# A transformer block on one core: another order of the work in a unit of attention heads

## The chip, the cores and the metric

The kernel runs on one core of a Trainium2 chip. The metric is the device time of one execution in microseconds (us). Three runs of the kernel before gave 312.1, 312.3 and 313.58 us; the median is 312.3.

## The reference

The input x has shape (32, 32, 256), cond (32, 256). What is computed, in float32:

```
x = x + conv(x)                # depthwise causal convolution over 32 lags, the filter is cond
ada = cond @ ada_w + ada_b     # six parts: shift1, scale1, gate1, shift2, scale2, gate2
x1 = layernorm(x) * (1 + scale1) + shift1
q, k, v = x1 @ qkv_w + qkv_b   # 16 heads of 128
o = softmax(q @ k.T * 128**-0.5) @ v       # for each batch element, 32 tokens by 32
x = x + gate1 * (o @ out_w + out_b)
x2 = layernorm(x) * (1 + scale2) + shift2
x = x + gate2 * (gelu(x2 @ ffn_w1 + ffn_b1) @ ffn_w2 + ffn_b2)
```

The conditioned block's own residual enters twice: the result is the sum of the convolved x and the block's output.

## The kernel before

Channels lie on the partitions (2 tiles of 128), tokens along the free dimension; the 1024 tokens are worked in two halves of 512. Every engine has its own list of instructions, written out by hand in the order in which it runs them, and the engines meet at semaphores. An instruction that waits holds up all that stands behind it on its engine.

**Precision.** A product is made of three fast matmuls: each operand is split into a high part and a low part (the remainder), and low x high, high x low and high x high are summed (`three`, lines 943 to 947; `v_tile`, 949 to 956). For weights ScalarE writes the high part (`high_parts`, line 348) and GpSimd (POOL) the low part (`low_parts`, line 297); for activations ScalarE writes the high part and VectorE (DVE) the low one.

**Units.** The attention is worked in eight units U = 0 to 7: four groups of four heads for each half of the tokens. A unit has twelve projection tiles (`project`, line 958): 0 to 3 are q of the four heads, 4 to 7 k, 8 to 11 v for four blocks of 128 tokens. Each is six matmuls of 512 columns into one of three PSUM banks in turn (`PB[j % 3]`), and ScalarE copies it out (`evac`, line 404). Then come the scores of all four heads (`scores`, line 995), the softmax on DVE with the exponentials on ScalarE (`softmax_front`, `exps`, `softmax_probs`, `softmax_transpose`), and, inside the next unit, the attention of each head (`attend`, line 1007) and its share of the output projection (`out_proj`, line 1023). Between the two, ScalarE writes the head's output high part (`o_high`, line 431) and DVE the low part (`o_low`, line 668). Attention output has two banks, so heads 2 and 3 wait for the `o_low` of heads 0 and 1.

**What is fitted between.** Unit 0 is projected in two chunks while the second half's convolution still runs on DVE (`conv`, line 538, spread over units 0 to 2). Unit 1 also holds the rest of the product ada (`modulation`, `modulation_turned`). Units 3 and 5 hold a layernorm each, of 512 tokens: TensorE's `mean`, `var` and `spread` (lines 886, 904, 918), which share the scores' bank; DVE's `centre`, `scale_up`, `var_eps`, `norm`, `shift`; ScalarE's `squares` and `x1_high`; and POOL's `rstd` (line 301), on which `spread` waits. The mean takes its input in two parts, `mean_high` by ScalarE and `mean_low` by DVE. Unit 7 is followed by the first ffn layer (`ffn1`, line 1116; its gelu and high part are ScalarE's `hidden`, line 489; its low parts `hidden_low` go to DVE for odd tiles and to POOL for even ones). Among the ffn1 tiles stands the attention of unit 7, then the layernorm of the second half, `mean(4)`, which needs `residual(1)` (line 675) on DVE first.

**Weights.** SyncE issues their transfers in one order (lines 242 to 245): q, k, v of a unit and then its rows of out_w, each as soon as POOL has made the low parts of what lay in that place before.

The order of TensorE's work in a unit is in lines 1077 to 1114, and of its counterparts in 320 to 328 (POOL), 455 to 487 (ScalarE) and 722 to 826 (DVE).

Of the kernel before, what the change touches and what calls it, by code (L numbers as in the profile page):

```python
# [16 lines left out]
def cond_resid_block_kernel(nc, x, cond, ada_w, ada_b, qkv_w, qkv_b, out_w, out_b,  # L17
# [7 lines left out]
    CT = C // P  # L25
    INNER = out_w.shape[0]
    NH = INNER // P
    GH = 4
# [42 lines left out]
    with ExitStack() as ctx:  # L71
# [204 lines left out]
        def _(g):  # L276
# [43 lines left out]
            for U in range(1, NU):  # L320
                if U == 3:
                    rstd(2)
                if U == 5:
                    rstd(3)
                low_parts(U + 1, 0)
                low_parts(U + 1, 1)
                low_parts(U, 3)
                low_parts(U + 1, 2)
# [16 lines left out]
        def _(a):  # L345
# [109 lines left out]
            for U in range(1, NU):  # L455
                for j in range(4):
                    evac(U, j)
                if U == 1:

                    a.wait_ge(s_adap, 3)  # L460
                    a.wait_ge(s_adax, 1)
                    a.activation(ada_rows[:, :], S_BANK[:, 0:2 * P], ACT.Copy).then_inc(s_adac, 1)
                o_high(U - 1, 0)
                o_high(U - 1, 1)
                if U == 3:
                    squares(2)
                if U == 5:
                    squares(3)
                evac(U, 4)
                o_high(U - 1, 2)  # L470
                high_parts(U + 1, 0)
                o_high(U - 1, 3)
                if U == 3:
                    x1_high(2)
                if U == 5:
                    x1_high(3)
                for j in (5, 6, 7, 8):
                    evac(U, j)
                    if U in (2, 4) and j in (6, 7):
                        mean_high(U // 2 + 1, j - 6)  # L480
                high_parts(U + 1, 1)
                exps(U)
                evac(U, 9)
                high_parts(U, 3)
                evac(U, 10)
                evac(U, 11)
                high_parts(U + 1, 2)
# [11 lines left out]
            hidden(0, 0)  # L499
            hidden(0, 1)  # L500
            o_high(NU - 1, 0)
            hidden(0, 2)
            o_high(NU - 1, 1)
            hidden(0, 3)
            o_high(NU - 1, 2)
            o_high(NU - 1, 3)
            high_parts(NU, 3)
# [22 lines left out]
        def _(v):  # L530
# [195 lines left out]
            conv(1, 7, 9)  # L726
# [3 lines left out]
            conv(1, 9, 10)  # L730
            o_low(0, 2)
            conv(1, 10, 11)
            o_low(0, 3)
# [3 lines left out]
            conv(1, 11, 18)  # L737
# [3 lines left out]
            conv(1, 18, 20)  # L741
# [3 lines left out]
            conv(1, 20, 21)  # L745
            o_low(1, 2)
            conv(1, 21, 22)
            o_low(1, 3)
            conv(1, 22, len(DVE_LAGS[1]))
            mean_low(2)  # L750
            softmax_front(2)
            softmax_probs(2)
            softmax_transpose(2)

# [5 lines left out]
            o_low(2, 2)  # L760
            o_low(2, 3)
            norm(2)
            shift(2)
            x1_low(2)
            softmax_front(3)
# [5 lines left out]
            residual(0)  # L771
            mean_low(3)
            softmax_front(4)
            softmax_probs(4)
            softmax_transpose(4)

# [5 lines left out]
            o_low(4, 2)  # L782
            o_low(4, 3)
            norm(3)
            shift(3)
            x1_low(3)
            softmax_front(5)
# [5 lines left out]
            residual_sum(0)  # L793
            softmax_front(6)
            softmax_probs(6)
            softmax_transpose(6)

# [12 lines left out]
            hidden_low(0, 1)  # L810
            o_low(7, 0)
            o_low(7, 1)
            hidden_low(0, 3)
            o_low(7, 2)
            o_low(7, 3)
            residual(1)
# [39 lines left out]
        def _(pe):  # L856
# [216 lines left out]
            project_chunk(1, range(0, 5))  # L1073
            scores(0)
            project_chunk(1, (5,))

            for U in range(1, NU):

                ln = {3: 2, 5: 3}.get(U)
                if U == NG:  # L1080
                    pe.wait_ge(s_lo, CT * NC)
                project(U, range(0, 3))
                if U == 1:
                    pe.wait_ge(s_sd, U)
                    pe.wait_ge(s_adaw[1], 16)
                    modulation(1)
                    modulation(2)
                if ln:
                    pe.wait_ge(s_sd, U)
                    mean(ln)  # L1090
                project(U, (3,))
                attend(U - 1, 0)
                attend(U - 1, 1)
                project(U, (4,))
                if U == 1:
                    modulation_turned(1)
                    modulation_turned(2)
                attend(U - 1, 2)
                if ln:
                    var(ln)  # L1100
                out_proj(U - 1, 0)
                attend(U - 1, 3)
                out_proj(U - 1, 1)
                if ln:
                    spread(ln)
                out_proj(U - 1, 2)
                out_proj(U - 1, 3)
                project(U, (5, 6, 7, 8))
                if ln:
                    pe.wait_ge(s_mod, CT * (ln + 1))  # L1110
                if U == 1:
                    pe.wait_ge(s_adat, ADA_STEPS[2])
                scores(U)
                project(U, (9, 10, 11))
# [44 lines left out]
            ffn1(0, (0, 1, 2))  # L1159
            attend(last, 0)  # L1160
            attend(last, 1)
            ffn1(0, (3,))
            attend(last, 2)
            out_proj(last, 0)
            attend(last, 3)
            for h in (1, 2, 3):
                out_proj(last, h)
            ffn1(0, (4, 5, 6, 7))
# [63 lines left out]
```

## Time and profile before

| | |
|---|---|
| median of three runs | 312.3 us |
| profiled execution | 311.81 us |
| its span, first instruction to last | 310.0 us |
| TensorE busy | 298.0 us, 96% |
| VectorE busy | 180.2 us, 58% |
| ScalarE busy | 174.5 us, 56% |
| GpSimd busy | 120.4 us, 39% |

How to read it: PE is TensorE's matmuls, PEld its weight loads, DVE VectorE, ACT ScalarE, POOL GpSimd, SP SyncE. Matmuls are pipelined and their ends are modelled, so records of successive matmuls overlap, and the pace is read from their starts. L945 is line 945 of the kernel; a helper's line stands for all its calls. In timelines, like instructions in a row are merged into one with a count (x16), and an instruction before which the engine was idle has in brackets for how long and what released it.

### The profile page before, as it was taken

How to read it: one execution, taken by the hardware profiler on the slowest of the kernel's cores; microseconds unless marked ns; L12 is line 12 of the kernel's file. 1: busy time of each engine (PE TensorE's matmuls, PEld its weight loads, DVE VectorE, ACT ScalarE, POOL GpSimd, SP SyncE). 2: the span in 40 equal slices, each digit the busy share in tenths (PEclk: the TensorE clock that was granted, in tenths of full speed). 3: DMA queues.
4: the chain of work that ended last, by engine and by line, in shares of the span. 5: the costliest groups of instructions: out<-in, count | busy, mean ns of one | idle time of the engine just before them, and what ended most of it. 6: DMA issues, size and time to landing. Idle time of an engine off the chain costs nothing.

```text
span 310.0 us, 6149 instructions
## 1 busy us (share of the span) xinstructions
PE 298.0 (96%) x2604; PEld 251.9 (81%) x2604; DVE 180.2 (58%) x303; ACT 174.5 (56%) x316; POOL 120.4 (39%) x103
## 2 busy tenths in 40 slices
PE   4978999999999999999999999999999999899995
PEld 3875997878898888788888888888898888678885
DVE  3997698987866745472546554341620556957232
ACT  5752568434762855486376736644762794625901
POOL 5007729331911544072337305531821671611400
PEclk9999999999999999999999999999999999999999
DMA  7903321400160061007004300610150020000012
GB/s 231 362 27 79 112 84 57 150 0 2 43 231 0 2 229 45 0 4 271 1 2 153 120 2 2 213 59 2 59 212 2 2 68 3 0 0 3 0 68 68
DMA packets 15259, 23.00 MB, mean 74 GB/s; under 512 B 792, under 2 KB 8320, under 8 KB 15232
## 3 DMA queue, kind: packets, MB, share of 16 engines
q1 hardware_dynamic: 15184, 22.58, 21.6%
q8 instruction: 20, 0.33, 0.4%
q10 hardware_dynamic: 48, 0.03, 0.1%
q14 instruction: 7, 0.06, 0.1%
HBM read 21.57 MB, written 1.05 MB: 73 GB/s over the span
## 4 chain that ended last, share of the span: by engine, by line
PE 85%; DVE 9%; POOL 3%; ACT 1%; DMA 1%; issue 1%; DVEq 0%; POOLq 0%
PE bank L945 18%; PE bank L947 18%; PE bank L946 18%; PE bank L1019 9%; DVE xc L548 6%; PE bank L953 5%; PE bank L954 4%; PE bank L955 4%; PE bank L1003 3%; POOL wl L294 3%; PE bank L925 1%; DVE x1l L617 1%; PE bank L894 1%; DMA crow<-in_cond_dram 1%; PE bank L867 1%
## 5 line engine op out<-in xcount | busy, mean ns | idle before, releaser
L294 POOL TENSOR_TENSOR wl<-raw,wh 128x512 fp32r<-128x512 f32 x72 | 98.7, 1398 | 133.2 <-ACT wh L357 116.5
L408 ACT ACTIVATE pool<-bank,bT 128x512 f32<-128x512 f32 x56 | 38.5, 688 | 54.3 <-PE bank L947 54.3
L945 PE MATMUL bank<-x1h,wl 128*128 128x512 f32 (+1 forms) x176 | 66.3, 377 | 0.8 <-DVE x1l L623 0.4
L947 PE MATMUL bank<-x1h,wh 128*128 128x512 f32 (+1 forms) x176 | 65.1, 370 | 0.0
L946 PE MATMUL bank<-x1l,wh 128*128 128x512 f32 (+1 forms) x176 | 65.1, 370 | 0.0
L671 DVE SCALAR_TENSOR_TENSOR ol<-bank,bT,oh 128x512 fp32r<-128x512 f32 x32 | 24.0, 750 | 36.6 <-ACT oh L433 35.6
L357 ACT ACTIVATE wh<-raw 128x512 fp32r<-128x512 f32 x72 | 40.9, 621 | 3.5 <-PE bank L947 3.5
L548 DVE SCALAR_TENSOR_TENSOR xc<-x,condT,xc 128x496 f32<-128x496 f32 (+27 forms) x82 | 42.8, 592 | 0.1
L945 PEld LDWEIGHTS bank<-x1h,wl 128*128 128x128 f32 x176 | 33.2, 188 | 7.1 <-DVE x1l L623 0.8
L947 PEld LDWEIGHTS bank<-x1h,wh 128*128 128x128 f32 x176 | 33.2, 188 | 5.7
L946 PEld LDWEIGHTS bank<-x1l,wh 128*128 128x128 f32 x176 | 33.2, 189 | 5.4
L1019 PEld LDWEIGHTS bank<-pt,pool 128*128 128x128 f32 x256 | 32.1, 191 | 2.0 <-issue 0.3
L1019 PE MATMUL bank<-pt,pool 128*128 128x128 f32 x256 | 32.5, 275 | 0.0
L433 ACT ACTIVATE oh<-bank,bT 128x512 fp32r<-128x512 f32 x32 | 22.0, 686 | 10.0 <-PE bank L1019 10.0
L945 PE MATMUL bank<-oh,wl 128*128 128x512 f32 x64 | 26.8, 418 | 0.2 <-DVE ol L671 0.2
L953 PE MATMUL bank<-wh,x1l 128*128 128x512 f32 x64 | 25.9, 404 | 0.0
L947 PE MATMUL bank<-oh,wh 128*128 128x512 f32 x64 | 25.1, 392 | 0.0
L946 PE MATMUL bank<-ol,wh 128*128 128x512 f32 x64 | 25.0, 390 | 0.0
L954 PE MATMUL bank<-wl,x1h 128*128 128x512 f32 x64 | 24.9, 389 | 0.0
L955 PE MATMUL bank<-wh,x1h 128*128 128x512 f32 x64 | 24.9, 389 | 0.0
L643 DVE TENSOR_REDUCE mx<-bank 128x16 f32<-128x512 f32 x8 | 5.5, 692 | 32.4 <-PE bank L1003 32.4
L666 DVE STREAM_TRANSPOSE pt<-pnorm 32x512 f32<-32x512 f32 (+1 forms) x36 | 23.2, 644 | 1.2
(121 smaller groups left out, 421.5 us busy)
## 6 DMA issues: line engine op xcount, KB each, us to landing
raw<-in_L_cond_qkv_w_dram SPq DMA_DIRECT2D x24, 512.0 KB, 5.6
raw<-in_L_cond_out_w_dram SPq DMA_DIRECT2D x8, 512.0 KB, 3.7
raw<-in_L_cond_ffn_w_dram SPq DMA_DIRECT2D x4, 512.0 KB, 5.1
adaw<-in_L_cond_ada_w_dram SPq DMA_DIRECT2D x1, 1024.0 KB, 10.8
out_dram<-pool SPq DMA_DIRECT2D x3, 256.0 KB, 2.2
pool<-in_x_dram SPq DMA_DIRECT2D x2, 256.0 KB, 3.1
adaw<-in_L_cond_ada_w_dram SPq DMA_DIRECT2D x1, 512.0 KB, 5.4
pool<-in_x_dram SPq DMA_DIRECT2D x1, 512.0 KB, 6.2
```

The costliest lines, as they stand in the source:

```text
L294: g.tensor_tensor(wl[:, cols], raw[:, cols], wh[:, cols].bitcast(F32), ALU.subtract)\
L357: a.activation(wh[:, cols], raw[:, cols], ACT.Copy).then_inc(s_whi[i], 1)
L408: a.activation((q_sb if j < GH else k_sb)[:, j % GH, :], src, ACT.Identity, bias=bias(U, j // GH, j % GH)).then_inc(s_ev, 1)
L548: m = v.scalar_tensor_tensor(out=acc[:, :, j:], in0=xs[:, :, :T - j], scalar=w, in1=(acc if i else xs)[:, :, j:], op0=ALU.mult, op1=ALU.add)
L671: v.scalar_tensor_tensor(out=ol[:, h, :], in0=OB[h % 2][:, :], scalar=bT[:, row:row + 1], in1=oh[:, h, :].bitcast(F32), op0=ALU.add, op1=A ...
L945: pe.matmul(dst, wl[:, w_cols], a_hi, start=start, stop=False)
L946: pe.matmul(dst, wh[:, w_cols], a_lo, start=False, stop=False)
L947: return pe.matmul(dst, wh[:, w_cols], a_hi, start=False, stop=stop)
L953: pe.matmul(dst, x1l[:, kt, tk], wh[:, wc], start=(kt == 0), stop=False)
L954: pe.matmul(dst, x1h[:, kt, tk], wl[:, wc], start=False, stop=False)
L955: m = pe.matmul(dst, x1h[:, kt, tk], wh[:, wc], start=False, stop=(kt == CT - 1))
L1019: m = pe.matmul(OB[h % 2][:, t * P:(t + 1) * P], v_sb[:, t, h * P:(h + 1) * P], pt[:, h, t, :], start=True, stop=True)
```

## The change

All of it is order; no operation is added or taken away, and no tile or semaphore changes.

- **TensorE, a unit:** attention of heads 2 and 3 of the last unit moves behind projection tile 7, directly ahead of this unit's scores; the output projection of all four heads stands in one piece behind the scores; v's tiles 8 to 11 come last. `mean` stands behind tile 3, `var` behind tile 4, `spread` behind tile 6. In unit 0 the scores stand behind the fourth tile of the second chunk, not the fifth. In the last part, ffn1's tiles 1 and 2 stand between heads 0, 1 and heads 2, 3, and tiles 3 to 7 behind the output projection.
- **ScalarE:** the same order for its copies; `mean_high` moves into units 3 and 5, behind `evac` of tiles 0 and 1; `squares` stands between `o_high` of heads 0 and 1; `exps` ahead of the k weights' high parts; in unit 1 the copy of ada's rows stands behind `evac` 5.
- **DVE:** in units 3 and 5 `o_low` of heads 2 and 3 stands behind the layernorm; `residual(0)` and `mean_low(3)` behind the softmax of unit 4, `mean_low(2)` behind that of unit 2; `hidden_low(0, 3)` ahead of `residual(1)`.
- **POOL:** `low_parts(U + 1, 0)` stands ahead of `rstd`.

```
@@ POOL
             for U in range(1, NU):
+                low_parts(U + 1, 0)
                 if U == 3:
                     rstd(2)
                 if U == 5:
                     rstd(3)
-                low_parts(U + 1, 0)
                 low_parts(U + 1, 1)
                 low_parts(U, 3)
                 low_parts(U + 1, 2)
@@ ScalarE
                 for j in range(4):
                     evac(U, j)
-                if U == 1:
-                    a.wait_ge(s_adap, 3)
-                    a.wait_ge(s_adax, 1)
-                    a.activation(ada_rows[:, :], S_BANK[:, 0:2 * P], ACT.Copy).then_inc(s_adac, 1)
+                    if U in (3, 5) and j < CT:
+                        mean_high((U + 1) // 2, j)
                 o_high(U - 1, 0)
-                o_high(U - 1, 1)
                 if U == 3:
                     squares(2)
                 if U == 5:
                     squares(3)
+                o_high(U - 1, 1)
                 evac(U, 4)
-                o_high(U - 1, 2)
                 high_parts(U + 1, 0)
-                o_high(U - 1, 3)
+                evac(U, 5)
+                if U == 1:
+                    a.wait_ge(s_adap, 3)
+                    a.wait_ge(s_adax, 1)
+                    a.activation(ada_rows[:, :], S_BANK[:, 0:2 * P], ACT.Copy).then_inc(s_adac, 1)
+                evac(U, 6)
+                evac(U, 7)
                 if U == 3:
                     x1_high(2)
                 if U == 5:
                     x1_high(3)
-                for j in (5, 6, 7, 8):
-                    evac(U, j)
-                    if U in (2, 4) and j in (6, 7):
-                        mean_high(U // 2 + 1, j - 6)
+                o_high(U - 1, 2)
+                o_high(U - 1, 3)
+                exps(U)
                 high_parts(U + 1, 1)
-                exps(U)
+                evac(U, 8)
                 evac(U, 9)
                 high_parts(U, 3)
...
             hidden(0, 0)
+            o_high(NU - 1, 0)
+            o_high(NU - 1, 1)
             hidden(0, 1)
-            o_high(NU - 1, 0)
-            hidden(0, 2)
-            o_high(NU - 1, 1)
-            hidden(0, 3)
             o_high(NU - 1, 2)
             o_high(NU - 1, 3)
+            hidden(0, 2)
+            hidden(0, 3)
             high_parts(NU, 3)
@@ DVE
-            conv(1, 7, 9)
+            conv(1, 7, 8)
             o_low(0, 0)
             o_low(0, 1)
-            conv(1, 9, 10)
-            o_low(0, 2)
-            conv(1, 10, 11)
-            o_low(0, 3)
+            conv(1, 8, 10)
             modulation(1)
             modulation(2)
             one_plus(2, SCALE2)
-            conv(1, 11, 18)
+            conv(1, 10, 11)
+            o_low(0, 2)
+            o_low(0, 3)
             softmax_front(1)
...
             centre(2)
             o_low(2, 0)
             o_low(2, 1)
             scale_up(2)
             var_eps(2)
-            o_low(2, 2)
-            o_low(2, 3)
             norm(2)
             shift(2)
             x1_low(2)
+            o_low(2, 2)
+            o_low(2, 3)
...
-            hidden_low(0, 1)
             o_low(7, 0)
             o_low(7, 1)
-            hidden_low(0, 3)
+            hidden_low(0, 1)
             o_low(7, 2)
             o_low(7, 3)
+            hidden_low(0, 3)
             residual(1)
             mean_low(4)
@@ TensorE
-            project_chunk(1, range(0, 5))
+            project_chunk(1, range(0, 4))
             scores(0)
-            project_chunk(1, (5,))
+            project_chunk(1, (4, 5))
...
-                project(U, range(0, 3))
+                project(U, range(0, 4))
...
                     mean(ln)
-                project(U, (3,))
                 attend(U - 1, 0)
                 attend(U - 1, 1)
                 project(U, (4,))
+                if ln:
+                    var(ln)
+                project(U, (5, 6))
                 if U == 1:
                     modulation_turned(1)
                     modulation_turned(2)
-                attend(U - 1, 2)
-                if ln:
-                    var(ln)
-                out_proj(U - 1, 0)
-                attend(U - 1, 3)
-                out_proj(U - 1, 1)
                 if ln:
                     spread(ln)
-                out_proj(U - 1, 2)
-                out_proj(U - 1, 3)
-                project(U, (5, 6, 7, 8))
+                project(U, (7,))
+                attend(U - 1, 2)
+                attend(U - 1, 3)
...
                 scores(U)
-                project(U, (9, 10, 11))
+                for h in range(GH):
+                    out_proj(U - 1, h)
+                project(U, (8, 9, 10, 11))
...
-            ffn1(0, (0, 1, 2))
+            ffn1(0, (0,))
             attend(last, 0)
             attend(last, 1)
-            ffn1(0, (3,))
+            ffn1(0, (1, 2))
             attend(last, 2)
-            out_proj(last, 0)
             attend(last, 3)
-            for h in (1, 2, 3):
+            for h in range(GH):
                 out_proj(last, h)
-            ffn1(0, (4, 5, 6, 7))
+            ffn1(0, (3, 4, 5, 6, 7))
             mean(4)
```

## Rows read from the trace of the kernel before

**Rows 1.** The page, part 1: busy time, share, instructions of each engine.
```profile
PE 298.0 (96%) x2604; PEld 251.9 (81%) x2604; DVE 180.2 (58%) x303; ACT 174.5 (56%) x316; POOL 120.4 (39%) x103
```

**Rows 2.** Stretches: units 2 and 3; length, busy times, granted clock, DMA share, GB/s.
```profile
80.56:107.34 26.78, 26.78 (x257) 22.57 (x256) 18.73 (x38) 16.05 (x27) 10.70 (x9) 1.00 0.24 80
107.34:136.79 29.45, 29.45 (x286) 24.80 (x285) 15.50 (x26) 17.25 (x30) 11.62 (x10) 1.00 0.21 73
```

**Rows 3.** Timeline of TensorE in unit 3: start, us, what.
```profile
113.55 0.39 PE L947 MATMUL bank<-x1h,wh 128*128 128x512 f32 x1
113.78 1.95 PE L1019 MATMUL bank<-pt,pool 128*128 128x128 f32 x16
115.48 0.48 PE L945 MATMUL bank<-x1h,wl 128*128 128x512 f32 x1
115.79 0.40 PE L946 MATMUL bank<-x1l,wh 128*128 128x512 f32 x1
116.03 0.39 PE L947 MATMUL bank<-x1h,wh 128*128 128x512 f32 x1
...
122.27 1.05 PE L925 MATMUL bank<-ident,rs 128*128 128x128 f32 x8
```

**Rows 4.** Timeline of ScalarE in unit 3.
```profile
114.87 0.69 ACT L433 ACTIVATE oh<-bank,bT 128x512 fp32r<-128x512 f32 x1 [0.20 <-PE bank L1019]
115.76 0.69 ACT L433 ACTIVATE oh<-bank,bT 128x512 fp32r<-128x512 f32 x1 [0.21 <-PE bank L1019]
116.35 1.14 ACT L388 ACTIVATE x<-yacc 128x512 f32<-128x512 f32 x2
...
118.61 1.14 ACT L357 ACTIVATE wh<-raw 128x512 fp32r<-128x512 f32 x2
```

**Rows 5.** Timeline of DVE in unit 3.
```profile
112.62 1.28 DVE L578 TENSOR_TENSOR yacc<-xc,bank 128x512 f32<-128x512 f32 x2 [2.52 <-PE bank L894]
115.59 1.65 DVE L671 SCALAR_TENSOR_TENSOR ol<-bank,bT,oh 128x512 fp32r<-128x512 f32 x2 [1.69 <-ACT oh L433]
117.15 1.28 DVE L585 TENSOR_TENSOR yacc<-yacc,adaT 128x512 f32<-128x512 f32 x2
...
118.98 0.17 DVE L597 TENSOR_SCALAR ve<-vt 128x4 f32<-128x4 f32 x1
```

**Rows 6.** Timeline of POOL in unit 3.
```profile
119.23 1.01 POOL L304 TENSOR_TENSOR rs<-ve,mhalf 128x4 f32<-128x4 f32 x1 [7.16 <-DVE ve L597]
120.21 2.53 POOL L294 TENSOR_TENSOR wl<-raw,wh 128x512 fp32r<-128x512 f32 x2
```

**Rows 7.** Line L585 by itself (ns min/median/max), and DVE and POOL at 262 us.
```profile
L585 DVE TENSOR_TENSOR yacc<-yacc,adaT x6: 412/684/1487, 25.2 to 117.7; 128x256 f32<-128x256 f32 x4, 128x512 f32<-128x512 f32 x2
...
262.23 2.39 DVE L685 TENSOR_TENSOR yacc<-yacc,xc 128x512 f32<-128x512 f32 x2
...
262.33 3.44 POOL L294 TENSOR_TENSOR wl<-raw,wh 128x512 fp32r<-128x512 f32 x2 [6.67 <-ACT wh L357]
```

**Rows 8.** Timelines of ScalarE and TensorE around the scores of unit 0.
```profile
47.45 0.83 ACT L420 ACTIVATE pool<-bank,bT 128x256 f32<-128x256 f32 x2
...
48.40 1.30 PE L1003 MATMUL bank<-pool 128*32 128x32 f32 x128
...
51.61 0.50 PE L945 MATMUL bank<-x1h,wl 128*128 128x512 f32 x1 [0.35 <-POOL wl L294]
```

**Rows 9.** Timelines of DVE and TensorE in unit 1.
```profile
64.29 3.08 DVE L548 SCALAR_TENSOR_TENSOR xc<-x,condT,xc 128x352 f32<-128x352 f32 x2
...
68.08 0.50 PE L945 MATMUL bank<-oh,wl 128*128 128x512 f32 x1 [0.18 <-DVE ol L671]
```

**Rows 10.** Timelines of ScalarE and TensorE ahead of mean(4).
```profile
262.92 0.69 ACT L494 ACTIVATE pool<-bank,bT 128x512 f32<-128x512 f32 x1
...
264.18 1.14 ACT L393 ACTIVATE x1h<-yacc 128x512 fp32r<-128x512 f32 x2
...
268.15 0.70 PE L894 MATMUL bank<-x1h,ones_r 128*128 128x512 f32 x2 [1.19 <-DVE x1l L617]
```

**Rows 11.** The page, part 6: size of a transfer, us from issue to landing.
```profile
raw<-in_L_cond_qkv_w_dram SPq DMA_DIRECT2D x24, 512.0 KB, 5.6
```

More of the change, by code:

```diff
@@ L457, in _ @@
                     evac(U, j)
+                    if U in (3, 5) and j < CT:
+                        mean_high((U + 1) // 2, j)
+                o_high(U - 1, 0)
+                if U == 3:
+                    squares(2)
+                if U == 5:
+                    squares(3)
+                o_high(U - 1, 1)
+                evac(U, 4)
+                high_parts(U + 1, 0)
+                evac(U, 5)
                 if U == 1:
@@ L462, in _ @@
                     a.activation(ada_rows[:, :], S_BANK[:, 0:2 * P], ACT.Copy).then_inc(s_adac, 1)
-                o_high(U - 1, 0)
-                o_high(U - 1, 1)
[L465 to L469, printed above, removed]
-                o_high(U - 1, 2)
-                high_parts(U + 1, 0)
-                o_high(U - 1, 3)
+                evac(U, 6)
+                evac(U, 7)
                 if U == 3:
@@ L740, in _ @@
             softmax_transpose(1)
-            conv(1, 18, 20)
+            conv(1, 11, 20)
             o_low(1, 0)
             o_low(1, 1)
-            conv(1, 20, 21)
+            conv(1, 20, 25)
             o_low(1, 2)
-            conv(1, 21, 22)
             o_low(1, 3)
-            conv(1, 22, len(DVE_LAGS[1]))
-            mean_low(2)
             softmax_front(2)
@@ L753, in _ @@
             softmax_transpose(2)
+            conv(1, 25, len(DVE_LAGS[1]))
+            mean_low(2)
             centre(2)
@@ L770, in _ @@
                 o_low(3, h)
-            residual(0)
-            mean_low(3)
             softmax_front(4)
@@ L775, in _ @@
             softmax_transpose(4)
+            residual(0)
+            mean_low(3)
             centre(3)
@@ L781, in _ @@
             var_eps(3)
-            o_low(4, 2)
-            o_low(4, 3)
             norm(3)
@@ L786, in _ @@
             x1_low(3)
+            o_low(4, 2)
+            o_low(4, 3)
             softmax_front(5)
@@ L792, in _ @@
                 o_low(5, h)
-            residual_sum(0)
             softmax_front(6)
@@ L796, in _ @@
             softmax_transpose(6)
+            residual_sum(0)
             for h in range(GH):
```

## The prediction

> **What bounds the kernel.** I read the busy shares first [rows 1]: TensorE is busy 96% of the span, no other engine above 58%. Then stretches of one unit each [rows 2]: an ordinary unit is 26.78 us long and TensorE is busy for all of it; a unit with a layernorm piece lasts 29.45 us, busy throughout; the granted clock is 1.00 (2.4 GHz) in both. Then TensorE's own timeline in unit 3 [rows 3]: two 512-column matmuls follow each other at 0.23 us (115.79 to 116.03), so a projection tile, an output-projection head or an ffn1 tile (six matmuls) takes 1.36 us. The attention of two heads takes 115.79 - 113.55 - 2 x 0.227 = 1.79 us, 0.90 a head. The scores take 1.44 us: 26.78 less twelve tiles and four heads of output projection (16 x 1.36), and less four heads of attention (3.58). So the loop has no idle time to win. TensorE waits only at a few edges, and a change of order can pay only there; everywhere else it can only open waits.
>
> The waits that there are: a recorded idle time counts from a modelled end, 0.39 after a matmul's start where the next starts after 0.23, so 0.16 is added, and 0.11 where the first matmul behind it takes 0.50. That gives 0.62 us for weight low parts before unit 1 [rows 8], 0.45 in unit 1 for o_low of head 3 [rows 9], and 1.35 ahead of mean(4), behind the last unit [rows 10]: 2.4 us together.
>
> **Units without a layernorm piece.** The same matmuls in another order; what each waits for is earlier than its new place. I count t from a unit's first tile. In the changed order tiles 0 to 3 end at 5.44, attention 0 and 1 at 7.23, tile 4 at 8.59, 5 and 6 at 11.31, 7 at 12.67, attention 2 and 3 at 14.46, scores at 15.90, output projection at 21.34, tiles 8 to 11 at 26.78. ScalarE takes a finished tile 0.20 us later and needs 0.69 [rows 4], so k's last tile is copied at 13.56, before the scores at 14.46. o_high and o_low of head 3 end near 15.4 and 16.2; the output projection of head 3 starts at 19.98. The softmax gets more time than before: the next attention is 16 us behind the scores, where it was 10. Joining heads 2, 3 and the scores gives nothing back, since the 26.78 us are full. What a change between the kinds of matmul costs I bound by the 0.09 us by which the first behind attention is recorded longer (0.48 for 0.39): term 0, bounds -0.6 and +0.6 for seven units.
>
> The weights' transfers are a matter of SyncE's order: the q transfer for unit U+1 is queued behind the o transfer, which waits for POOL's low_parts(U-1,3), and that moves with tile 9 to the end of unit U-1. In unit 3 it is issued about t = 2.4 and lands in 5.6 us [rows 11], at about 8; its first reader, high_parts(4,0), comes at 10.3. Term 0, but the cover is only 2 us.
>
> **Start and unit 1.** scores(0) moves ahead of chunk 1's fifth tile, and needs the evacuation of its fourth. ScalarE has high_parts(1,0) ahead of that, so the evacuation runs 47.45 to 48.28, and the scores start at 48.40 even now [rows 8]. They can't come earlier; the fifth tile (1.36 us) that fills this time now follows them, so unit 1 is reached 1.36 us later, less the 0.62 us wait for low parts, which are then ready: +0.74. In unit 1 the copy of ada_rows moves behind the evacuation of tile 4, high_parts(2,0) and the evacuation of tile 5 (0.20 + 0.6 + 1.0 + 0.6 behind tile 4), and with the copy, taken as half an evacuation, ends just after TensorE has made two more tiles (2.72) and wants to turn it: +0.1. The wait for o_low 3, caused by a conv pair of 3.08 us ahead of it, goes: -0.45. Term: +0.4, bounds -0.5 (the scores' wait goes unpaid) and +1.5.
>
> **Units 3 and 5, the largest term.** Here mean, var and spread stand between the tiles, and two edits make a chain that was covered late: PE's order, and on POOL low_parts(U+1,0) ahead of rstd. With t from the unit's first tile:
> - tiles 0 to 3 to 5.44; mean to 6.35; attention 0 and 1 to 8.14; tile 4 to 9.50; var (0.8) to 10.3; tiles 5 and 6 to 13.0: this is where spread stands. Before, two tiles and three heads of attention stood between mean and var (5.4 us; now a tile and two heads, 3.15), and two heads of output projection and one of attention between var and spread (3.6; now two tiles, 2.7).
> - ScalarE [rows 4]: o_high 0 starts 1.09 after the first attention (114.87 less 113.78), 7.44; squares 8.03 to 9.17 (centre ends 1.5 after mean [rows 5], 7.85, in time); o_high 1 9.07 to 9.76; evacuation of tile 4 9.70; high_parts(U+1,0) at 10.29, its first half at 10.9.
> - DVE [rows 5]: o_low 0 8.2; o_low 1 9.8 to 10.5; scale_up from 10.46, two operations at 0.6; var_eps behind it.
> - POOL [rows 6]: low_parts(U+1,0) can start at 10.99; its two operations take 2.53 alone. rstd (1.01) now stands behind them; before it stood ahead (119.23, then 120.21).
>
> Alone, POOL ends the low parts at 13.52 and rstd at 14.5: spread waits 1.6 us. But they collide with scale_up. What the rows show: L585, the same operation, takes 0.68, its half-size form 0.41, and once 1.49, where POOL subtracts beside it; the residual's two additions take 2.39 for 2 where 1.3 is usual, with POOL's low parts beside them [rows 7]. So each of the two waits for the other's whole operation: scale_up 0 to 11.1, low part 1 to 12.4, scale_up 1 to 13.0, low part 2 to 14.3, rstd to 15.3, spread at 15.4 in place of 13.0. The wait is 2.4 us in each of two units: +4.8. Bounds: +0.7, if POOL came to rstd as soon as ve is there (scale_up ends 11.8 alone, ve 12.2, rstd 13.3, spread 0.35 late, twice), and +7, if the weights came late and POOL held rstd behind them (another 1 us each). Behind spread nothing more is late: norm needs 1.5 us, tile 7 and two heads cover 3.15. The mean itself is close: mean_high now runs in this unit, and mean_low 1, which may wait for POOL's low_parts(U,2), ends near 5.3 for 5.44.
>
> The Trainium skill (SBUF: State Buffer, "Who interferes with whom") says that a DVE instruction with two SBUF inputs and a GpSimd instruction that reads SBUF exclude each other for the whole instruction, the first to start winning. That speaks against this change; by it the term is 4.8, and if two inputs did not contend it would be 3.2. The trace sides with the rule, by the row of L585.
>
> **The last unit.** I count from ffn1's first tile. Before, tile 3 stands ahead of attention 2; now tiles 3 to 7 stand behind the output projection. Tile 0, two heads, two tiles, two heads and the output projection end at 13.1; tile 3 at 14.5; its gelu and copy run from 14.7 to 16.1 (262.92 to 264.18 is the same pair [rows 10]). On DVE hidden_low(0,3) stands ahead of residual(1) and needs this copy; before, the residual began as soon as the output projection ended. So: hidden_low to 16.8, the two gating operations to 18.1, the two additions with POOL's low_parts(8,3) beside them (first half ready at 16.7, since high_parts(8,3) also stands behind hidden(0,3)) to 20.7, mean_high 1 to 21.3, mean_low to 23.2 with hidden_low of POOL beside it; mean at 23.3. TensorE has finished tile 7 at 20.0: a wait of 3.3 in place of 1.35. Term: +1.9; bounds -0.5 (nothing collides: mean at 20.9) and +3.
>
> **Sum.** 0.4 + 4.8 + 1.9 = 7.1 us on a profiled execution of 311.81 us (span 310.0 and 1.8 around it): 318.9. The median of the three runs is 0.5 above the profiled one: I say **319.0 us**.
>
> **Rivals.**
> - *The collisions don't bite.* POOL's operations slip between DVE's. For it: the middle record of L585 is 0.68 although POOL is busy 39% of the span. Against: the one at 1.49 [rows 1, 7]. 0.4 + 3.2 + 0 = 3.6: 315.5 us. Chance 0.2.
> - *The waits are longer.* POOL's low parts wait for a late q transfer with rstd behind them, or the clock falls in a wait of 2 to 3 us (the page shows full speed through the wait of 1.35; each us at 1.2 GHz would cost half a us). 2 to 4 us more: 321 to 323. Chance 0.1.
> - *Nothing changes.* TensorE stays full since rstd is in time after all. For it: before, spread had 2.0 us to spare (rstd ends at 120.24, spread starts at 122.27) [rows 3, 6]. Against: the new order takes more than that. 311.5 to 313. Chance 0.08.
> - *Faster.* One mechanism: the waits of before are closed by the tiles now behind them and none opens. It decides at ScalarE's high_parts(U+1,0): if POOL's low parts were through before var, near 10, rstd would be free; they would have to start 3.5 us earlier than I place them. Price: -2.4 us, 310. Chance 0.07.
>
> **How the numbers follow.** Forecast 0.55, its own range 317.2 to 320.5. A measurement tells 0.5% (1.6 us) from no change. Slower holds the forecast and the first two rivals, 0.85; no change 0.08; faster 0.07. The range goes down to the rival without collisions and up into the longer waits: 314.3 to 321.6; what lies outside is no change, faster and the upper part of the second rival, 0.2.
>
> **What would show it.** Right: in units 3 and 5 spread (L925) waits for POOL's rs by 2 to 2.5 us, POOL does two wl operations right ahead of rs, one scale_up takes 1.5 us or more; scores(0) waits 1.3 us for ScalarE's evacuation; mean(4) waits about 3.3 us for x1l, and residual(1) starts only after hidden_low(0,3). Wrong: rs ready ahead of spread; a TensorE wait in ordinary units, or ahead of every scores; or the loop's unit shorter than 26.78 us.

## The result

The changed kernel takes 320.38 us (median of 4, 319.86 to 321.41), the kernel before 312.25 (median of 4): ratio 1.026, 95% interval 1.0237 to 1.0283. Slower, as forecast; 319.0 was said, in a range of 314.3 to 321.6. Ratios here and below leave out executions over 1.5% longer than the fastest of the same kernel; that concerns two of e3's six.

### The profile page after: what moved, and what is told of

It is laid out like the page before. It is cut to its first block, busy times and chain, and to the rows that moved or that the text cites. A ratio compares the mean times of both kernels' runs of the same rounds, so it can differ in the third digit from the quotient of the medians.

```text
span 318.0 us, 6149 instructions
## 1 busy us (share of the span) xinstructions
PE 301.0 (95%) x2604; PEld 254.7 (80%) x2604; DVE 189.9 (60%) x303; ACT 173.8 (55%) x316; POOL 122.8 (39%) x103
## 4 chain that ended last, share of the span: by engine, by line
PE 82%; DVE 11%; ACT 3%; POOL 2%; DMA 1%; issue 1%; DVEq 0%; POOLq 0%
PE bank L945 18%; PE bank L946 17%; PE bank L947 17%; PE bank L1019 9%; DVE xc L550 5%; PE bank L953 5%; PE bank L955 5%; PE bank L954 5%; PE bank L1003 3%; PE bank L925 1%; POOL wl L294 1%; DVE yacc L687 1%; PE bank L894 1%; POOL rs L304 1%; ACT oh L433 1%; DMA crow<-in_cond_dram 1%
## 5 line engine op out<-in xcount | busy, mean ns | idle before, releaser
L294 POOL TENSOR_TENSOR wl<-raw,wh 128x512 fp32r<-128x512 f32 x72 | 101.0, 1426 | 147.0 <-ACT wh L357 130.3
L550 DVE SCALAR_TENSOR_TENSOR xc<-x,condT,xc 128x496 f32<-128x496 f32 (+27 forms) x82 | 44.5, 615 | 0.1
L411 ACT ACTIVATE pool<-bank 128x512 f32<-128x512 f32 x28 | 16.7, 596 | 34.6 <-PE bank L955 34.6
L1019 PEld LDWEIGHTS bank<-pt,pool 128*128 128x128 f32 x256 | 30.9, 191 | 1.7 <-issue 0.6
L1019 PE MATMUL bank<-pt,pool 128*128 128x128 f32 x256 | 31.3, 275 | 0.0
L945 PE MATMUL bank<-oh,wl 128*128 128x512 f32 x64 | 25.8, 403 | 0.0
L953 PE MATMUL bank<-wh,x1l 128*128 128x512 f32 x64 | 25.0, 391 | 0.0
```

The source lines that it names most:

```text
L294: g.tensor_tensor(wl[:, cols], raw[:, cols], wh[:, cols].bitcast(F32), ALU.subtract)\
L550: m = v.scalar_tensor_tensor(out=acc[:, :, j:], in0=xs[:, :, :T - j], scalar=w, in1=(acc if i else xs)[:, :, j:], op0=ALU.mult, op1=ALU.add)
L945: pe.matmul(dst, wl[:, w_cols], a_hi, start=start, stop=False)
L953: pe.matmul(dst, x1l[:, kt, tk], wh[:, wc], start=(kt == 0), stop=False)
L1019: m = pe.matmul(OB[h % 2][:, t * P:(t + 1) * P], v_sb[:, t, h * P:(h + 1) * P], pt[:, h, t, :], start=True, stop=True)
```

## The profile after

The profiled execution took 319.86 us, its span 318.0, 8.0 more than before. First the page: the span and the busy shares.

```profile
span 318.0 us, 6149 instructions
PE 301.0 (95%) x2604; PEld 254.7 (80%) x2604; DVE 189.9 (60%) x303; ACT 173.8 (55%) x316; POOL 122.8 (39%) x103
```

The instructions are as many on every engine as before [rows 1]; TensorE is busy 3.0 us longer and idle 5.0 us longer. So 5 us are waits; the other 3 are longer records of the same matmuls: 1.6 at a lower clock behind the last unit, as the third stretch below shows, and 1.1 in the convolution's matmuls at the start (L881, 17.1 before and 18.2 now), which cost nothing, since the first v tile comes no later. The longest waits of TensorE (in total, times, longest):

```profile
PE bank L925 <- POOL rs L304: 4.2, 3, 1.9
...
PE bank L894 <- DVE x1l L619: 2.9, 1, 2.9
PE bank L1003 <- ACT pool L420: 1.3, 1, 1.3
```

The stretches by unit (columns as in [rows 2]): unit 2, unit 3 and the first 3.5 us of ffn2.

```profile
80.95:107.75 26.80, 26.80 (x257) 22.85 (x257) 23.09 (x44) 15.12 (x25) 12.59 (x10) 1.00 0.23 80
107.75:139.50 31.75, 29.84 (x286) 24.78 (x286) 19.90 (x27) 18.06 (x32) 12.16 (x10) 1.00 0.20 68
275.50:279.00 3.50, 3.50 (x10) 2.72 (x9) 2.99 (x5) 3.07 (x6) 1.29 (x1) 0.51 0.00 0
```

An ordinary unit is as long and as full as before; unit 3 has about 2 us in which TensorE stands. In the third row it is busy throughout, but at half its clock: 0.51 of full speed, that is, at the lower of its two levels (1.2 and 2.4 GHz).

Taken between the same instructions of both traces, the 8.0 us are: ahead of the first v tile of chunk 0 (TensorE's first L953, at 38.41 before and 38.33 after) -0.1; from it to unit 1 +0.82 (13.20 to 14.02); unit 1 -0.50; units 2, 4, 6 and 7 -0.10 together; unit 3 +2.20, unit 5 +2.39; unit 7's end to ffn2 +1.76; ffn2 to the end +1.56.

**Unit 3.** ScalarE, then DVE, then POOL, then TensorE, from each one's timeline (start, length, what, idle time before):

```profile
117.29 0.69 ACT L408 ACTIVATE pool<-bank,bT 128x512 f32<-128x512 f32 x1
117.87 1.14 ACT L357 ACTIVATE wh<-raw 128x512 fp32r<-128x512 f32 x2
```
```profile
117.36 0.75 DVE L673 SCALAR_TENSOR_TENSOR ol<-bank,bT,oh 128x512 fp32r<-128x512 f32 x1 [0.86 <-ACT oh L433]
118.02 2.39 DVE L587 TENSOR_TENSOR yacc<-yacc,adaT 128x512 f32<-128x512 f32 x2
120.34 0.30 DVE L596 STREAM_TRANSPOSE vt<-bank 128x128 f32<-128x128 f32 x1
120.68 0.90 DVE L599 TENSOR_SCALAR ve<-vt 128x4 f32<-128x4 f32 x1
```
```profile
118.57 2.98 POOL L294 TENSOR_TENSOR wl<-raw,wh 128x512 fp32r<-128x512 f32 x2 [7.05 <-ACT wh L357]
121.66 1.01 POOL L304 TENSOR_TENSOR rs<-ve,mhalf 128x4 f32<-128x4 f32 x1
```
```profile
122.72 1.16 PE L925 MATMUL bank<-ident,rs 128*128 128x128 f32 x8 [1.91 <-POOL rs L304]
```

POOL's two low parts start 0.55 us after DVE's scale_up and run beside it: scale_up takes 2.39 where it took 1.28 [rows 5], the low parts 2.98 where they took 2.53 [rows 6], and the reciprocal root (L304) stands behind both. Spread waits 1.91 as recorded, 2.07 by the reading of the prediction, which adds 0.16 to a recorded wait. The 0.90 us of ve, 0.17 before [rows 5], also end only when POOL's second low part does, at 121.6.

**Behind the last unit.** DVE, POOL, ScalarE and TensorE:

```profile
267.75 0.69 DVE L807 TENSOR_TENSOR hl<-pool,hh 128x512 fp32r<-128x512 f32 x1 [6.74 <-ACT hh L499]
268.36 1.40 DVE L682 SCALAR_TENSOR_TENSOR yacc<-bank,bT,adaT 128x512 f32<-128x512 f32 x2
269.68 3.42 DVE L687 TENSOR_TENSOR yacc<-yacc,xc 128x512 f32<-128x512 f32 x2
273.02 1.47 DVE L619 TENSOR_TENSOR x1l<-yacc,x1h 128x512 fp32r<-128x512 f32 x2
```
```profile
268.31 2.55 POOL L294 TENSOR_TENSOR wl<-raw,wh 128x512 fp32r<-128x512 f32 x2 [5.48 <-ACT wh L357]
270.82 1.73 POOL L332 TENSOR_TENSOR hl<-pool,hh 128x512 fp32r<-128x512 f32 x1
```
```profile
267.08 0.63 ACT L499 ACTIVATE hh<-pool 128x512 fp32r<-128x512 f32 x1
...
273.13 0.63 ACT L393 ACTIVATE x1h<-yacc 128x512 fp32r<-128x512 f32 x1 [1.06 <-DVE yacc L687]
```
```profile
274.63 0.70 PE L894 MATMUL bank<-x1h,ones_r 128*128 128x512 f32 x2 [2.87 <-DVE x1l L619]
275.17 0.68 PE L894 MATMUL bank<-x1l,ones_r 128*128 128x512 f32 x2
275.64 0.63 PE L945 MATMUL bank<-hh,wl 128*128 128x512 f32 x1
276.07 0.63 PE L946 MATMUL bank<-hl,wh 128*128 128x512 f32 x1
```

DVE has been idle for 6.74 us when it does hidden_low(0,3) (L807), because that waits for ScalarE's copy (L499) at 267.7; the residual (L682, L687) queues behind it, though its heads were ready (in e2 below it starts at 264.42), and its two additions then meet POOL's second low part and POOL's hidden_low (L332): 3.42 us. Mean(4) waits 3.03 (1.35 before [rows 10]). On DVE hidden_low(0,3) stood ahead of residual(1) in the kernel before too, but there its tile came ahead of attention 2. It is TensorE's move of tile 3 behind the output projection that made the copy late. From 275.64 on, 1 us behind the wait's end, the matmuls follow at 0.43 us, not 0.23: the clock has fallen. Eight do so: 8 x 0.2 = 1.6 us, the +1.56.

**Start.** The scores of unit 0 on TensorE:

```profile
48.25 1.30 PE L1003 MATMUL bank<-pool 128*32 128x32 f32 x128 [1.26 <-ACT pool L420]
```

The 1.26 us are the ScalarE evacuation that was foreseen.

## The experiments

The time of an execution varies with the stretch ahead of the first v tile and with the clock (the kernel before alone took 311.72 to 314.56 us in the 57 executions taken beside these runs); where a wait decides I read it in the trace, and lengths from the first v tile on. Ratios are to the kernel before on the same chip.

**1. e1_rstd_first: POOL's order alone undone.**
```
 for U in range(1, NU):
-    low_parts(U + 1, 0)
     if U == 3: rstd(2)
     if U == 5: rstd(3)
+    low_parts(U + 1, 0)
```


> The changed kernel with one edit undone: POOL's rstd stands ahead of low_parts(U+1,0) again. Theory (POOL's order holds rstd, and its low parts beside scale_up make ve late as well): POOL is idle until ve, which comes at about 119.8 instead of 121.6; rstd ends near 120.9, spread waits about 0.3 us instead of 2.07 in units 3 and 5, and the time falls by 3.5 us to about 316.9. Rival (TensorE's order alone brings var and spread too early; ve is late by DVE's own chain, rstd only follows it): the waits stay near 2 us and the time near 320.4.

Measured: 317.06 us, ratio 1.0141 (1.0103 to 1.018). DVE, POOL and TensorE in unit 3:
```profile
120.60 1.28 DVE L587 TENSOR_TENSOR yacc<-yacc,adaT 128x512 f32<-128x512 f32 x2
...
122.14 0.17 DVE L599 TENSOR_SCALAR ve<-vt 128x4 f32<-128x4 f32 x1
```
```profile
122.39 1.01 POOL L304 TENSOR_TENSOR rs<-ve,mhalf 128x4 f32<-128x4 f32 x1 [8.30 <-DVE ve L599]
123.37 2.52 POOL L294 TENSOR_TENSOR wl<-raw,wh 128x512 fp32r<-128x512 f32 x2
```
```profile
123.45 1.16 PE L925 MATMUL bank<-ident,rs 128*128 128x128 f32 x8
```
The root comes as soon as ve is there, scale_up and ve are short again, and spread stands only 0.33 us longer than its neighbours (0.45 - 0.23 after the last matmul's start, 0.11 in the first behind it). So POOL's place for the root, and the collision it brings, hold nearly all of this term; units 3 and 5 stay 0.35 and 0.56 longer than before.

**2. e4_before_low_first: the same edit put into the kernel before.**
```
 for U in range(1, NU):
+    low_parts(U + 1, 0)
     if U == 3: rstd(2)
     if U == 5: rstd(3)
-    low_parts(U + 1, 0)
```


> The kernel before with one edit of the change: low_parts(U+1,0) ahead of rstd on POOL. Theory (the price of POOL's order depends on how much stands between var and spread on TensorE, 3.6 us here): high_parts allow the first low part at 119.3, rstd starts near 121.9 and ends near 122.9, spread, due at 122.27, waits 0.6 to 0.7 us in units 3 and 5; the time rises by 1.3 us to about 313.6. Rivals: POOL's order by itself costs the whole 2.1 us a unit (316.4), or nothing, since TensorE's order is all (312.3).

Measured: 313.73 us, ratio 1.005 (1.0026 to 1.0075). Spread in unit 3:
```profile
122.94 1.16 PE L925 MATMUL bank<-ident,rs 128*128 128x128 f32 x8 [0.44 <-POOL rs L304]
```
Recorded 0.44 is 0.6 of wait, and the unit is 0.7 longer: that is what POOL's edit costs in the old order. The rest of the change without it (e10) makes units 3 and 5 longer by 0.35 and 0.55, both together by 2.2 and 2.4, about twice the sum. TensorE's new order has taken the cover: spread was due 14.8 us after the unit's first tile, 2.0 behind the end of the root; now it is due at 13.1.

**3. e5_no_collision: scale_up ahead of o_low 1, so that it is through before POOL starts.**
```
 o_low(2, 0)
-o_low(2, 1)
 scale_up(2)
+o_low(2, 1)
 var_eps(2)
```
(and the same for norm 3 in unit 5)

> The changed kernel with scale_up ahead of o_low of head 1 in units 3 and 5, so that it is over before POOL's low_parts(U+1,0) begin; POOL's order stays as changed. Theory (the two low parts and scale_up exclude each other, and that is part of the wait): the low parts take 2.54 us instead of 2.98, scale_up 1.28 for two instead of 2.39, rstd starts about 0.55 us earlier, spread waits 1.5 us instead of 2.07, twice: 1.1 us less, 319.3. Rival (the low parts alone hold rstd, the collision costs nothing on the path): the wait stays at 2.07.

Measured: 317.99 us, ratio 1.0159 (1.0112 to 1.0205); 317.18 in the runs whose clock stayed at 1.0. DVE, POOL, TensorE:
```profile
117.40 1.28 DVE L587 TENSOR_TENSOR yacc<-yacc,adaT 128x512 f32<-128x512 f32 x2
...
119.60 1.28 DVE L599 TENSOR_SCALAR ve<-vt 128x4 f32<-128x4 f32 x1
```
```profile
119.56 2.54 POOL L294 TENSOR_TENSOR wl<-raw,wh 128x512 fp32r<-128x512 f32 x2 [7.06 <-ACT wh L357]
```
```profile
123.12 1.16 PE L925 MATMUL bank<-ident,rs 128*128 128x128 f32 x8 [1.32 <-POOL rs L304]
```
The wait is 1.48 instead of 2.07: the collision is worth 0.6 of each wait, the queue alone 1.5 (1.6 was said). Units 3 and 5 are each 0.6 us shorter than in the changed kernel; the medians, 2.4 apart, hold other executions with other clocks as well. Ve takes 1.28 beside POOL's first low part, but ends before the second does: what is left is the queue on POOL.

**4. e2_hidden_low_later: the residual no longer behind hidden_low(0,3).**
```
-hidden_low(0, 3)
 residual(1)
 mean_low(4)
+hidden_low(0, 3)
```


> The changed kernel with hidden_low(0,3) behind mean_low(4) instead of ahead of residual(1). Theory (the residual starts late because hidden_low(0,3) waits ahead of it): the residual starts near 264.2 instead of 268.4, its additions no longer meet POOL, mean_high follows hidden(0,4) at 269.9, and the last mean_low still meets POOL: the wait ahead of mean(4) falls from 3.03 to between 0.6 and 2.0 us. If the clock falls only behind a wait as long as 3 us, it stays at 1.00 and another 1.5 us goes: 316.5 to 318. Rival (ScalarE's order, mean_high behind hidden(0,4), sets the wait anyway): the wait stays above 2.5 and the time within 0.5 us of 320.4.

Measured: 316.94 us, ratio 1.0156 (1.0117 to 1.0195). DVE, TensorE, and the 3.5 us behind mean(4):
```profile
264.42 1.43 DVE L682 SCALAR_TENSOR_TENSOR yacc<-bank,bT,adaT 128x512 f32<-128x512 f32 x2 [3.33 <-PE bank L947]
265.76 1.28 DVE L687 TENSOR_TENSOR yacc<-yacc,xc 128x512 f32<-128x512 f32 x2
270.64 2.54 DVE L619 TENSOR_TENSOR x1l<-yacc,x1h 128x512 fp32r<-128x512 f32 x2 [3.60 <-ACT x1h L393]
```
```profile
273.33 0.70 PE L894 MATMUL bank<-x1h,ones_r 128*128 128x512 f32 x2 [1.48 <-DVE x1l L619]
```
```profile
274.20:277.70 3.50, 3.50 (x30) 2.53 (x28) 2.77 (x5) 2.42 (x4) 1.34 (x1) 1.00 0.00 0
```
The residual starts 3.9 us earlier and collides no more, the wait falls from 3.03 to 1.64, and the clock stays at 1.00 where the changed kernel had 0.51. Between the two profiled executions, 2.9 us apart, 1.4 is wait and 1.6 clock; the medians are 3.4 apart. What is left of the wait is ScalarE's order: mean_high(4) stands behind hidden(0,4), and mean_low then meets POOL.

**5. e3_fill_the_wait: the wait ahead of mean(4) filled with work.** Twelve matmuls whose result nobody reads.
```
 ffn1(0, (3, 4, 5, 6, 7))
+for _ in range(12):
+    pe.matmul(OB[1][:, :], ones_r[:, :], x1h[:, 0, 0:HT], start=True, stop=True)
 mean(4)
```


> The changed kernel with twelve extra matmuls of 512 columns ahead of mean(4), into a bank that nobody reads before it is overwritten: TensorE works through 2.7 us of the 3.03 us wait; nothing else changes. Theory (the wait lowers TensorE's clock, and the matmuls behind mean(4) pay for it): the granted clock stays 1.00 behind mean(4), the eight matmuls at 0.43 us go back to 0.23, ffn2 starts when it did, and the time falls by 1.5 us to about 318.9 although TensorE does more. Rival (the clock falls for another reason there, by its own time): the slow stretch stays, and the time is 320.4 or more.

Measured: 321.14 us (318.36 to 323.86), ratio 1.024 (1.0194 to 1.0287): missed in the median, where a fall of 1.5 us was expected. The fastest run, the one whose mean clock was 1.0, took 318.36. In the profile no slow matmul follows mean(4), but there are slow ones behind the wait of spread in unit 3, where the changed kernel's profile has none. That stretch, and TensorE in it:
```profile
123.00:127.50 4.50, 3.62 (x14) 3.14 (x15) 2.17 (x4) 0.00 (x0) 0.82 (x1) 0.68 0.00 2
```
```profile
123.88 1.42 PE L925 MATMUL bank<-ident,rs 128*128 128x128 f32 x8 [1.91 <-POOL rs L304]
...
125.52 0.63 PE L946 MATMUL bank<-x1l,wh 128*128 128x512 f32 x1
125.95 0.63 PE L947 MATMUL bank<-x1h,wh 128*128 128x512 f32 x1
```
Unit 3 is 1.6 us longer for it than in the changed kernel (33.26 for 31.65). So the fall behind mean(4) hangs on the wait: it comes in all four profiles that have the wait of 2.86 or 2.87 there (the changed kernel, e1, e5, e8) and in neither that fills it (e3, e7). A wait of 2.07 us is paid for with the clock in one execution and not in another.

**6. e7_fill_all_waits: as e3, and eight such matmuls ahead of spread in units 3 and 5.**
```
 if ln:
+    pe.wait_ge(s_ev, UB * U + 5)
+    for _ in range(8):
+        pe.matmul(PB[1][:, :], ones_r[:, :], x1h[...], start=True, stop=True)   # x1h's columns left out
     spread(ln)
```


> The changed kernel with the three waits filled by extra matmuls: twelve ahead of mean(4) as before, and eight (1.8 us) ahead of spread in units 3 and 5, into a bank whose old content has been read. Theory (each of the waits can lower the clock, now one, now another, so that filling one alone did not help every execution): the clock stays 1.00 in nearly all executions and the time is 318.4, with executions within 0.5 us but for the start. Rival (the clock falls on its own): clock 0.984 to 0.995 in most executions and 320 to 321 as before.

Measured: 320.53 us, ratio 1.0254 (1.0219 to 1.029): missed in time. The clock did what was expected in four of the six executions (a mean of 0.998 to 1.0; the changed kernel's four have 0.987 to 0.992). The filled waits are gone in the profile, but unit 5 has one that no other profile shows, with a fall of the clock behind it; together they make it 3.5 us longer. DVE, then TensorE:
```profile
186.53 1.40 DVE L673 SCALAR_TENSOR_TENSOR ol<-bank,bT,oh 128x512 fp32r<-128x512 f32 x2
```
```profile
188.90 0.47 PE L945 MATMUL bank<-oh,wl 128*128 128x512 f32 x1 [1.85 <-DVE ol L673]
...
190.21 0.63 PE L947 MATMUL bank<-oh,wh 128*128 128x512 f32 x1
```
DVE's o_low, to which the wait is put down, had ended at 187.93, 0.97 us earlier, so it is not what TensorE waited for. Why the wait is there, and whether the other executions have it, stays open; so this run does not settle what filled waits are worth.

**7. e8_scores_back: the start alone undone.**
```
-project_chunk(1, range(0, 4))
+project_chunk(1, range(0, 5))
 scores(0)
-project_chunk(1, (4, 5))
+project_chunk(1, (5,))
```


> The changed kernel with scores(0) back behind the fifth tile of chunk 1. My theory: the 1.3 us wait of the scores for ScalarE's evacuation goes, the 0.62 us wait for weight low parts before unit 1 comes back, so unit 1's first tile comes 0.6 to 0.7 us earlier and the median falls from 320.4 to 319.7. Rival (the fifth tile is paid for in another place, since the start of the two kernels differs by 0.3 us only): no change, 320.4, and unit 1 starts where it did.

Measured: 321.51 us, ratio 1.0275 (1.0231 to 1.0318): the median did not fall. In the trace the step is as said: the scores no longer wait, the weight's wait is back (0.32 recorded at 53.80), and from the first v tile to unit 1 it takes 13.19 us, as before (13.20), not 14.02. But this execution came to that v tile 2.28 us later, ahead of every edited instruction of TensorE, its clock was low there too (0.66 granted from 28 to 33 us), and it fell behind spread in unit 3 (five matmuls at 0.43). The 0.8 us are seen in the trace alone; the time cannot show them.

**8. e10_three_undone: e1, e2 and e8 together.** The diff is the sum of theirs.

> The changed kernel with three of its edges undone together: rstd ahead of low_parts(U+1, 0) on POOL, hidden_low(0, 3) behind mean_low(4) on DVE, scores(0) behind the fifth tile. My theory: these three hold all of the loss (3.3, 3.4 with the clock, 0.7), and the rest of the change, the whole new order of the units, costs nothing: 313.0, within 0.3% of the kernel before (312.6). Rival (the order itself costs): 314.5 or more, with the units longer than 26.80 us or a wait of spread over 0.5 us left.

Measured: 312.59 us, ratio 1.0007 (0.9985 to 1.0029): no difference from before. So three edges hold the loss; two of them are undone, the third, hidden_low(0,3), is put where it was not before either. From the first v tile to the end it is 272.3 us against 271.6 before: 0.9 more in units 3 and 5 (the 0.33 of e1 among it), 0.4 at mean(4), 0.4 less in unit 1, 0.1 less in the ordinary units. With these edges mended, the order that the change is named after costs and gives nothing that the times can show.

**9. e9_before_tail: the kernel before, one edge mended.**
```
 high_parts(NU, 3)
-hidden(0, 4)
 mean_high(4, 0)
 mean_high(4, 1)
+hidden(0, 4)
```


> The kernel before, with ScalarE's mean_high(4, 0) and (4, 1) ahead of hidden(0, 4). Question: does the gain of the mended kernel (310.8 against 312.6) come from the new order, or from this place alone? My theory: from this place. The copy of tile 4 is made later, so POOL's hidden_low(0, 4) no longer runs beside the two subtractions of mean_low(4): these take 2.1 us instead of 3.18, mean(4) waits 0.2 to 0.4 us instead of 1.35, the time is 311.2 (1.1 less). Rival (the new order itself gains): mean(4) still waits over 1 us and the time stays at 312.3.

Measured: 312.17 us, ratio 0.9981 (0.996 to 1.0002). DVE and TensorE:
```profile
266.78 2.38 DVE L617 TENSOR_TENSOR x1l<-yacc,x1h 128x512 fp32r<-128x512 f32 x2
```
```profile
268.15 0.50 PE L945 MATMUL bank<-x1h,wl 128*128 128x512 f32 x1 [0.30 <-ACT pool L494]
...
269.64 0.62 PE L894 MATMUL bank<-x1h,ones_r 128*128 128x512 f32 x2
```
Mean(4) no longer waits, but the last ffn1 tile now waits 0.46 + 0.11 for ScalarE's later gelu, and mean_low took 2.38, not 2.1. From the first v tile on: 271.1 against 271.6. Half of the 1.1 that was expected, and the interval just reaches 1.

**10. e6_repaired: the new order with every wait mended** (run ahead of e8, e9 and e10).
```
 # beside the edits of e1, e2 and e8
+var_eps(n) ahead of scale_up(n)            # DVE, norms 2 and 3
+high_parts(NU, 3) ahead of hidden(0, 3)    # ScalarE, last unit
+mean_high(4, 0..1) ahead of hidden(0, 4)   # ScalarE, last unit
+high_parts(1, 0) one evacuation earlier    # ScalarE, start
```


> The changed kernel's order of heads, scores and output projection with the edits that cost time undone or moved: rstd ahead of low_parts; var_eps ahead of scale_up in units 3 and 5; hidden_low(0,3) behind mean_low(4); on ScalarE high_parts(NU,3) ahead of hidden(0,3) and mean_high(4) ahead of hidden(0,4); scores(0) behind the fifth tile of the chunk again, and high_parts(1,0) one tile earlier. Theory (TensorE's order in a unit costs nothing by itself, only the waits do): no wait of TensorE above 0.2 us behind the start, a unit of 26.8 us, units 3 and 5 of 29.5, and the waits of before (0.62, 0.45 and 1.35) gone too: a span of 307.7 us, 309.5 us in all, 0.9% under the kernel before. Rival (the new order itself costs time): 312 or more.

Measured: 310.76 us against 312.64, ratio 0.9937 (0.9915 to 0.9959): it is faster than both, though 1.3 us short of the 309.5 expected. From the first v tile to the end 270.0 us, 1.5 less than before; mean(4) and the spreads record no wait:
```profile
121.20 1.05 PE L925 MATMUL bank<-ident,rs 128*128 128x128 f32 x8
...
267.86 0.62 PE L894 MATMUL bank<-x1h,ones_r 128*128 128x512 f32 x2
```
The 0.62 us for the weights at unit 1 did not go with the earlier high_parts. Of the gain 1.4 us lie between unit 7's end and ffn2, where e9 in the old order gains 0.8; so the gain is mostly that of mended waits and not of the order of the units.

## Why the prediction was right

Each step by what it measured, in the profiled execution:

- *Ordinary units, 0*: -0.10 for four of them. Right; in e10 they are 26.80 as well.
- *Start and unit 1, +0.4*: +0.82 and -0.50, together +0.3. The scores wait for the evacuation as said (1.26 against 1.3), o_low's 0.45 is gone.
- *Units 3 and 5, +4.8*: +4.59. In unit 3 scale_up was placed at 10.46 and the low parts at 10.99 after the unit's first tile; they came at 10.44 and 10.99. Spread was placed at 15.4 and came at 15.1. The turns were right and each a little too long. The rows above merge the operations; one by one, the second scale_up took 1.80 (0.68 alone) and ended 0.55 behind the first low part, and the second low part took 1.72 (1.28 alone) and ended 1.13 behind that scale_up: 12.3, 12.8 and 14.0 where 12.4, 13.0 and 14.3 were said. So the wait was 2.07 rather than 2.4. The two waits make 4.2 of the 4.59; where in these units the other 0.4 lies was not traced. Missed was that ve is caught too; it cost nothing, for POOL was busy until 121.6 anyway. (The 1.49 of [rows 7] was the half-size form, 0.41 alone, so the row said more for a collision than was read from it.)
- *The last unit, +1.9*: +1.76; the wait is 3.03, not 3.3. e2 shows the cause. Here two errors cancelled, which is luck: the residual's additions ended 0.9 us later than said, because POOL's hidden_low met the second of them, and so it did not meet mean_low, which ended 0.7 behind mean_high and not 1.9.
- *The clock*: not in the sum; it stood in the second rival, at half a us for each slow us. It is +1.56 in the profiled execution, which took 319.86 where 318.9 was said: without it the forecast would have come out 0.6 too long. That the total came so near is thus in part luck. The three other executions took 0.5 to 1.6 us more at a lower mean clock (0.987 to 0.989 for 0.992); what they lost, and where, no trace shows. Of that rival the price of a slow us was right (eight matmuls, 1.6 us in all, not the 2 to 4 of the rival), and the chance of 0.1 for the clock too low: "the page shows full speed through the wait of 1.35" says nothing on a wait of 3.

The rivals: no collision is refuted by the 2.39 of scale_up and by e5; no change and faster by the 2.07 of spread: the high parts that decide the faster one started at 117.87, t = 10.3, as placed.

What the collision is: both inputs of scale_up lie in SBUF (yacc and adaT), and it is 1.28 alone (e1, e5) and 2.39 beside POOL's subtraction; the residual's first operation (L682), which reads one input from a PSUM bank, is 1.40 for two beside POOL's low parts and 1.43 in e2 without them. The Trainium skill (SBUF — State Buffer, "Who interferes with whom") gives both: two SBUF inputs contend with a GpSimd instruction that reads SBUF, one doesn't. Here the traces agree, by these four numbers. The same section of the Trainium skill says that tensor_scalar can enter a mode that takes both ports and then contends as well, which I had not used. The traces agree: ve, of 128x4 elements, is 0.17 alone, 0.90 and 1.28 beside POOL (the changed kernel, e5), and ends with POOL's operation in both.

## What to carry to other kernels

When an order is changed on two engines at once, price the edges in pairs: POOL's edit cost 0.7 us a unit and the rest of the order 0.35 to 0.55, together 2.2 to 2.4, because the later place of spread had been the cover of POOL's root. Put the short operation that the bottleneck waits for (here a root of 1.01 us) ahead of long ones that nobody waits for yet, on every in-order engine, and keep two-input operations of DVE off the stretch in which POOL subtracts. A wait of TensorE like those of this case, of 1.85 to 2.87 us as recorded, is not priced by its length alone: add the slow matmuls behind it as a term with a chance.

## What the runs showed of the hardware

- The clock's fall goes with the length of TensorE's wait, and with chance. In the twelve profiles, from 40 us on, it fell behind all four recorded waits of 2.86 to 2.87 us, behind three of nine of 1.85 to 1.93 (unit 3 in e3 and e8, unit 5 in e7), and behind none of twelve of 1.19 to 1.48. These are counts of this case and no rule: two executions of e5, which has a wait of 2.86 in its profile, ran at a mean clock of 1.0. Each fall cost 1.3 to 1.6 us.
- A DVE operation on four elements a partition takes five to over seven times its 0.17 us where POOL's operation runs beside it (0.90 in the changed kernel, 1.28 in e5).
- The stretch ahead of the first v tile, where these kernels don't differ on TensorE, ended between 38.33 and 40.93 us (the latter in e1). It is a source of scatter of the size of most effects here, and it goes with TensorE's pace. The first convolution matmul came at 6.2 to 6.4 us in all twelve profiles. In e1, e3, e6 and e8 the first 24 took 8.23 us and the eight transposes behind them 1.62 to 1.93, elsewhere 6.2 to 7.5 and 1.06; in e5, e8, e9 and e10 the granted clock was 0.59 to 0.66 in a stretch of 5 us between 23 and 33 us, elsewhere 1.00. These seven came to the v tile at 39.19 or later, the other five at 38.33 to 38.45. Lengths taken from a fixed instruction on were steadier: 13.19 to 13.20 us to unit 1 in the six kernels that have the old start or have it back (before, e4, e6, e8, e9, e10).
